# A graph-attention and expert kernel: the scatter products of a chunk are spread 0, 2, 3, 3 over its units, and the last chunk is gathered by pairs of tiles with identity products between them

## The chip, the cores and the metric

The kernel runs on one core of a Trainium2 chip. The metric is device time in microseconds (us) of one execution, as the median of several runs. TensorE (PE in the profile) does the matrix products, with its weight loads shown apart (PEld); VectorE (DVE), ScalarE (ACT) and GpSimd (POOL) do elementwise work; SyncE's queue (SPq) issues nearly all DMAs. All DMAs of the core share 16 DMA engines.

## What is computed

```
x = x + gnn(layernorm(x))                 # x: 32 batches x 256 rows x 256
x = x + ffn(layernorm(x))
gnn: 8-head attention with adjacency mask, output projection, bias
ffn: rows in groups of 16; 64 expert slots (16 experts x 4 sets), 32 wide
  logits = grouped @ controller + tie           # 16 x 64 per group
  perm   = (logits == max over the 16 rows)     # one-hot, per group and slot
  inner  = relu(sum over rows of (grouped @ f1) * perm)
  inter2 = inner @ f2                           # per group and slot: 256 numbers
  result = sum over slots of inter2 * perm      # back to the rows
```

## The kernel before

The first two thirds of the time are the attention, batch by batch. The change touches only the second part, the experts. Its 8192 rows are 64 tiles of 128 rows, in 4 chunks of 16 tiles; a chunk is 4 units of 4 tiles.

**A unit** (`unit`, L714) prepares the experts' input. For one of its four tiles, `select` (L650) multiplies the normalised rows with the one-hot matrix, so that each expert slot gets the row it has chosen; DVE and ACT each copy half of the result out of four PSUM banks (L246, `save_selected`), and the next `select` waits for both copies, since it writes the same banks. In between TensorE does work for later units: `unit_transpose` (L546, two units ahead), `one_hot_transpose` (L566, the next unit) and `logits` (L559, two units ahead). DVE turns the logits into the one-hot matrices (L1067, L1074, L1086).

**The experts** of a chunk (`experts`, L736) are 16 steps of `expand` (L661, with f1) and `contract` (L682, with f2). The result of a step (512 KB) is copied to one of 5 slots of `stage` (DVE L1246, ACT L918) and written to `scratch` in DRAM by `move` (L325), where it lies by group.

**The scatter** brings it back to the rows. The chunk's result is read from `scratch` in another order, by expert slot and for one tile at a time: `gather(c, tile)` (L335, 512 KB per tile, 16 tiles) loads into the same 5 slots. `scatter(c, s)` (L709) multiplies the two tiles 2s and 2s+1 with the transposed one-hot matrices, into the one bank 3, and `finish` (L1204, DVE) adds the result to X, after which `store` (L341) writes it to the output. Eight scatters, s = 0 to 7, serve a chunk. For chunks 0 to 2 they run inside the units of the following chunk; the function `scatters(u)` says which s belong to unit u. Inside a unit the first stands after `select` 0, the second after `select` 2 and, where there is one, the third after `select` 3. DVE has the first `finish` ahead of the copy of `select` 1, the second ahead of the copy of `select` 3, and the third after the one-hot matrices of the unit.

Three waits tie this together. A tile from the sixth on is gathered only when the scatter that read its slot is done: tiles 5 and 6 after scatter 0, 7 and 8 after scatter 1, 9 and 10 after 2, 11 and 12 after 3, 13 and 14 after 4, tile 15 after scatter 5. A scatter after the first waits for the previous `finish`, since both use bank 3. And the one-hot matrices of a unit are written into a region of which the scatter of six units ago must be done. SyncE's queue has, in this order, the chunk's 16 moves, 16 gathers, 8 stores. So every store of a chunk and the first move of the next stand behind gather 15.

**The last chunk** has no following units. Its slots are not reused: `XRlast` holds all 16 tiles, loaded by 4 DMAs of 2 MB (L356), 4 tiles each. `scatter_last(s)` (L695) waits for its DMA where s is even, has four banks in turn, and `finish` and `store` follow.

Of the kernel before, what the change touches and what calls it, by code (L numbers as in the profile page):

```python
# [15 lines left out]
P = 128  # L16
# [7 lines left out]
def gnn_moe_kernel(nc, x, adj, Wq, bq, Wk, bk, Wv, bv, Wo, bo, controller, f1, f2, out):  # L24
# [11 lines left out]
    CT = 16  # L36
    CHUNKS = TILES // CT
    UT = 4
    UNITS = CT // UT
    GPT = P // T  # L40
    CG = CT * GPT
# [26 lines left out]
    with ExitStack() as ctx:  # L68
        def sb(name, shape, dt=F32):
            return ctx.enter_context(nc.sbuf_tensor(name, shape, dt))  # L70

        def sem(name):
            return ctx.enter_context(nc.semaphore(name))
# [7 lines left out]
        ident = sb("ident", [P, P])  # L81
# [66 lines left out]
        XRlast = nc.alloc_sbuf_tensor_at("XRlast", [P, CT, 4, D], F32, offset=floor)  # L148
# [4 lines left out]
        bank = [banks[:, i, :] for i in range(8)]  # L153
# [19 lines left out]
        bo_added = sem("bo_added")  # L173
        bias_ready, bias_done = sem("bias_ready"), sem("bias_done")
        root_done = sem("root_done")
        last_in = [sem(f"last_in{i}") for i in range(4)]
        hT_ready, hT_saved = sem("hT_ready"), sem("hT_saved")
        q_ready, q_saved = sem("q_ready"), sem("q_saved")
        k_ready, k_saved = sem("k_ready"), sem("k_saved")
# [69 lines left out]
        def out_bank(s):  # L249

            return bank[(7, 0, 1, 2)[s % 4]]

        def scatters(u):

            return ((), (0, 1, 2), (3, 4, 5), (6, 7))[u]

        def region(n):

# [2 lines left out]
        def chosen(tile, j):  # L261

            return permT[region(tile // UT)][:, (tile % UT * 4 + j) * 32:(tile % UT * 4 + j) * 32 + 32]
# [10 lines left out]
        def uses_of_slot(s):  # L274

            return (QUADS - s + SLOTS - 1) // SLOTS
# [11 lines left out]
        def _(sp):  # L288
# [62 lines left out]
                move(CHUNKS - 1, q)  # L351
            for i, m in enumerate(moved):
                sp.wait_ge(m, CHUNKS * uses_of_slot(i) * 16)
            for i in range(4):
                rows = slice((CHUNKS - 1) * CG + 4 * GPT * i, (CHUNKS - 1) * CG + 4 * GPT * (i + 1))
                sp.dma_start(XRlast[:, 4 * i:4 * i + 4, :, :].rearrange("p t j d -> p (t j) d"),  # L356
                             scratch[rows, :].rearrange("(c two) (e d) -> (two e) c d", two=2, d=D))\
                    .then_inc(last_in[i], 16)
            for s in range(CT // 2):
# [64 lines left out]
        def _(pe):  # L424
# [260 lines left out]

            def scatter_last(s):

                if s % 2 == 0:
                    pe.wait_ge(last_in[s // 2], 16)
                if s > 3:  # L690
                    pe.wait_ge(fin_done, (CHUNKS - 1) * (CT // 2) + s - 3)
                for tt in range(2):
                    for j in range(4):
                        tile = (CHUNKS - 1) * CT + 2 * s + tt
                        last = nc.tensor.matmul(out_bank(s)[32 * j:32 * j + 32, tt * D:tt * D + D],  # L695
                                                chosen(tile, j), XRlast[:, 2 * s + tt, j, :],
                                                start=True, stop=True)
                last.then_inc(sc_ready, 1)
# [15 lines left out]
            def unit(c, u):  # L714

                n = c * UNITS + u
                ahead = n + AHEAD < CHUNKS * UNITS
                pairs = scatters(u) if c > 0 else ()
                if ahead:
                    unit_transpose(n + AHEAD)  # L720
                select(n, 0)
                if n + 1 < CHUNKS * UNITS:
                    one_hot_transpose(n + 1)
                if pairs:
                    scatter(c - 1, pairs[0])
                select(n, 1)
                if ahead:
                    logits(n + AHEAD)
                select(n, 2)
                if pairs:  # L730
                    scatter(c - 1, pairs[1])
                select(n, 3)
                if len(pairs) > 2:
                    scatter(c - 1, pairs[2])
# [15 lines left out]
                experts(c)  # L750
            for s in range(CT // 2):
                scatter_last(s)


        @block.scalar
# [171 lines left out]
        def _(dve):  # L927
# [279 lines left out]
            def unit(c, u):  # L1207
                n = c * UNITS + u
                ahead = n + AHEAD < CHUNKS * UNITS
                pairs = scatters(u) if c > 0 else ()  # L1210
                save_selected(c, u, 0)
                late_root_steps(c, u, 0)
                if pairs:
                    finish(c - 1, pairs[0])
                save_selected(c, u, 1)
                late_root_steps(c, u, 1)
                if ahead:
                    tied_logits(n + AHEAD)
                save_selected(c, u, 2)
                late_root_steps(c, u, 2)  # L1220
                if pairs:
                    finish(c - 1, pairs[1])
                if ahead:
                    group_maximum()
                save_selected(c, u, 3)
                late_root_steps(c, u, 3)
                if ahead:
                    one_hot(n + AHEAD)
                if len(pairs) > 2:
                    finish(c - 1, pairs[2])  # L1230
# [46 lines left out]
```

## Time and profile before

| | before |
|---|---|
| median of 3 runs | 808.16 us (806.3 to 810.27) |
| the profiled execution | 806.59 us, its span 804.8 us |
| granted TensorE clock, mean | 0.977 |
| PE, DVE, ACT, POOL busy | 90%, 76%, 71%, 16% |
| HBM read, written | 47.78 MB, 41.94 MB |
| first unit's transposes with gathers open to first `expand`: chunks 1, 2, 3 | 591.23 to 627.68, 649.75 to 685.95, 708.01 to 743.63 us |
| gathers of the last chunk issued; last instruction of DVE starts | 770.65; 801.51 us |

The profiled execution took 1.8 us beyond its span, and lies 1.6 us under the median. The span is the time from the first to the last instruction; all times below are counted from its start. "Idle before <-releaser" in brackets says how long the engine stood idle ahead of an instruction and whose end released it. [...]

### The profile page before, as it was taken

Reading aid. Unit: us, or ns where it says so; the run is one execution under the profiler, and the core shown is the slowest. Engines: PE = TensorE matmul, PEld = TensorE weight load, DVE = VectorE, ACT = ScalarE, POOL = GpSimd, SP = SyncE. Lnnn points to the kernel's source line nnn. Section 1 sums busy time; section 2 is a strip of 40 time slices with the busy share of each in tenths; the row PEclk is TensorE's granted clock in tenths of the full one; section 3 lists DMA queues with packets and bytes.
Section 4 is the critical chain, followed back from the end, with each engine's and each line's share of the span. In section 5 each row is a group of like instructions: output and inputs, shape, how many; then the busy total and the mean of one; then the engine's idle time right before and its main releaser. Section 6 shows DMA issues by size and latency. Waiting matters only on the chain.

```text
span 804.8 us, 22451 instructions
## 1 busy us (share of the span) xinstructions
PE 728.1 (90%) x7252; PEld 556.7 (69%) x7252; DVE 612.7 (76%) x2558; ACT 568.3 (71%) x1654; POOL 125.4 (16%) x125
## 2 busy tenths in 40 slices
PE   4789999999999999999999999897888988986925
PEld 3578888888888888888888888765554555553602
DVE  2588998998988989989989989777656656655612
ACT  3499899899999998998998999765553453442500
POOL 1100100000010010001001003436425225200000
PEclk9899999999999999999999999999999999999956
DMA  6476656756765765666567466650589889889889
GB/s 157 105 170 144 160 136 154 172 137 138 171 155 121 170 155 133 161 154 154 139 154 171 112 138 140 151 204 2 211 312 339 329 312 334 338 304 345 345 303 303
DMA packets 102197, 157.60 MB, mean 196 GB/s; under 512 B 12288, under 2 KB 65024, under 8 KB 101888
## 3 DMA queue, kind: packets, MB, share of 16 engines
q1 hardware_dynamic: 99968, 155.56, 67.7%
q10 hardware_dynamic: 2176, 1.31, 0.7%
q8 instruction: 35, 0.57, 0.3%
q14 instruction: 18, 0.15, 0.1%
HBM read 47.78 MB, written 41.94 MB: 111 GB/s over the span
## 4 chain that ended last, share of the span: by engine, by line
PE 71%; DMA 14%; SPq 6%; DVE 5%; issue 2%; ACT 1%; ACTq 0%; DVEq 0%
PE bank L501 13%; PE bank L453 12%; DMA stage<-scratch 7%; PE bank L515 7%; PE bank L488 7%; PE bank L475 6%; PE bank L682 6%; PE bank L538 6%; PE bank L661 5%; SPq L301 4%; DMA XRlast<-scratch 2%; PE bank L446 2%; DMA scratch<-stage 2%; PE bank L650 2%; PE bank L709 2%
## 5 line engine op out<-in xcount | busy, mean ns | idle before, releaser
L826 ACT ACTIVATE Ps<-Ps,nmax 128x256 f32<-128x256 f32 x512 | 255.3, 503 | 23.4 <-DVE nmax L1015 21.7
L1015 DVE CUSTOM_DVE_ANT_0 Ps<-bank,masks 128x256 f32<-128x256 f32 x512 | 199.3, 420 | 27.2 <-issue 25.4
L501 PE MATMUL bank<-ident,Ps 128*128 128x128 f32 x1024 | 145.6, 275 | 2.0 <-DVE PTs L1026 1.5
L501 PEld LDWEIGHTS bank<-ident,Ps 128*128 128x128 f32 x1024 | 115.8, 140 | 20.2 <-issue 12.4
L453 PE MATMUL bank<-hT,WT 128*128 128x256 f32 x512 | 125.2, 389 | 0.8 <-ACT hT L783 0.8
L488 PE MATMUL bank<-stack 128*128 128x256 f32 x512 | 118.0, 332 | 6.2 <-DMA stack<-parts 6.0
L382 POOL TENSOR_TENSOR X<-X,bob 128x512 f32 (+1 forms) x32 | 40.8, 1277 | 431.5 <-ACT hn L791 431.5
L453 PEld LDWEIGHTS bank<-hT,WT 128*128 128x128 f32 x512 | 95.6, 196 | 12.2 <-issue 1.1
L826 ACT ACTIVATION_READ_ACCUMULATOR Ps<-Ps,nmax 128x1 f32 x512 | 98.1, 192 | 0.0
L394 POOL TENSOR_SCALAR h<-X,mv,roots 128x256 f32<-128x256 f32 x64 | 80.1, 1263 | 113.5 <-PE bank L650 85.7
L1026 DVE COPY PTs<-bank 128x512 f32<-128x512 f32 x128 | 87.7, 685 | 4.9 <-PE bank L501 4.8
L488 PEld LDWEIGHTS bank<-stack 128*128 128x128 f32 x512 | 80.5, 191 | 14.1 <-issue 5.0
L246 ACT COPY XS<-bank 128x512 f32<-128x512 f32 x64 | 37.8, 590 | 59.9 <-PE bank L650 59.9
L835 ACT COPY PTs<-bank 128x512 f32<-128x512 f32 x128 | 73.9, 577 | 0.4 <-PE bank L501 0.4
L809 ACT ACTIVATE parts<-bank,few 128x256 fp32r<-128x256 f32 x128 | 53.7, 471 | 26.3 <-PE bank L453 24.3
L515 PE MATMUL bank<-PTs,Vs 128*32 128x256 f32 x1024 | 68.5, 385 | 0.0
L918 ACT COPY stage<-bank 128x512 f32<-128x512 f32 x64 | 37.5, 587 | 42.9 <-PE bank L682 42.9
L1001 DVE SCALAR_TENSOR_TENSOR parts<-bank,few,parts 128x256 fp32r<-128x256 f32 x128 | 58.0, 479 | 8.4 <-ACT parts L809 8.4
L246 DVE COPY XS<-bank 128x512 f32<-128x512 f32 x64 | 44.6, 697 | 26.0 <-PE bank L650 25.9
L475 PE MATMUL bank<-WT,hT 128*128 128x256 f32 x256 | 61.9, 385 | 2.0 <-DVE parts L1001 1.8
L1204 DVE TENSOR_TENSOR X<-X,bank 128x512 f32<-128x512 f32 x32 | 22.0, 688 | 54.7 <-PE bank L695 31.1
L1246 DVE COPY stage<-bank 128x512 f32<-128x512 f32 x64 | 43.9, 691 | 25.1 <-PE bank L682 25.1
(84 smaller groups left out, 1028.8 us busy)
## 6 DMA issues: line engine op xcount, KB each, us to landing
stack<-parts SPq DMA_DIRECT2D x512, 128.0 KB, 2.4
scratch<-stage SPq DMA_DIRECT2D x64, 512.0 KB, 4.0
stage<-scratch SPq DMA_DIRECT2D x48, 512.0 KB, 6.2
X<-in_x SPq DMA_DIRECT2D x32, 256.0 KB, 2.8
out<-X SPq DMA_DIRECT2D x32, 256.0 KB, 4.7
XRlast<-scratch SPq DMA_DIRECT2D x4, 2048.0 KB, 15.9
f1s<-in_L_ffn_f SPq DMA_DIRECT2D x1, 2048.0 KB, 8.0
f2s<-in_L_ffn_f SPq DMA_DIRECT2D x1, 2048.0 KB, 13.9
```

Source lines behind the costliest of these rows:

```text
L246: return copy(XS[:, :, :, first:first + 4].rearrange("p k e (j two) -> p k e j two", two=2), banks[:, 4 + 2 * hf:6 + 2 * hf, 0:2 * P].rear ...
L394: last = nc.gpsimd.tensor_scalar(h2[n % NORMS][:, t, :], xtile(tile), mv2[:, tile, 0:1], roots[:, 1, tile:tile + 1], ALU.subtract, ALU.mult)
L453: last = nc.tensor.matmul(m[:, g * N:g * N + N], WT[:, w, k, g * P:g * P + P], hT[:, k, :], start=(k == 0), stop=(k == KT - 1))
L475: last = nc.tensor.matmul(M[0][:, t * D:t * D + D], hT[:, k, t * P:t * P + P], WT[:, 2, k, :], start=(k == 0), stop=(k == KT - 1))
L488: last = nc.tensor.matmul(s_bank(n)[:, h * N:h * N + N], stack[:, par, j, 0, g * N + t * P:g * N + t * P + P], stack[:, par, j, 1, g * N:g ...
L501: last = nc.tensor.transpose(PTb[h % 2][:, k * N + t * P:k * N + t * P + P], Ps[:, pr % 2, t, h % 2, k * P:k * P + P], ident[:, :])
L515: last = nc.tensor.matmul(Ob[32 * j:32 * j + 32, g * N:g * N + N], Vs[:, par, k, h * DH:h * DH + DH], PTs[:, h, k * N:k * N + N], start=(k ...
L826: last = nc.scalar.activation(Ps[:, pr % 2, t, h, :], Ps[:, pr % 2, t, h, :], ACT.Exp, bias=nmax[:, pr % 2, t, h:h + 1], scale=-1.0, accum ...
L835: nc.scalar.copy(PTs[:, h, :], PTb[h % 2][:, :]).then_inc(pt_act, 1)
L1001: low = nc.vector.scalar_tensor_tensor(parts[:, par, 2 * which + 1, g, :], M[1 - which][:, g * N:g * N + N], (bqs, bks)[which][:, g:g + 1] ...
L1015: last = nc.vector.tensor_tensor_reduce(out=Ps[:, pr % 2, t, h, :], in0=s_bank(n)[:, h * N:h * N + N], in1=masks[:, t, :], scale=1.0, scal ...
L1026: nc.vector.tensor_copy(PTs[:, h, :], PTb[h % 2][:, :]).then_inc(pt_dve, 1)
```

## The change

`scatters(u)` gives units 0 to 3 the scatters (), (0, 1), (2, 3, 4), (5, 6, 7) in place of (), (0, 1, 2), (3, 4, 5), (6, 7). `XRlast` is loaded by 8 DMAs of 1 MB, two tiles each, with a semaphore for each, and `scatter_last(s)` waits for its own. After each of the first seven of these scatters TensorE multiplies the identity matrix with itself 8 times, 128x128 by 128x128, into bank 5, which nothing reads any more.

```diff
-        last_in = [sem(f"last_in{i}") for i in range(4)]
+        last_in = [sem(f"last_in{i}") for i in range(CT // 2)]
...
-            return ((), (0, 1, 2), (3, 4, 5), (6, 7))[u]
+            return ((), (0, 1), (2, 3, 4), (5, 6, 7))[u]
...
-            for i in range(4):
-                rows = slice((CHUNKS - 1) * CG + 4 * GPT * i, (CHUNKS - 1) * CG + 4 * GPT * (i + 1))
-                sp.dma_start(XRlast[:, 4 * i:4 * i + 4, :, :].rearrange("p t j d -> p (t j) d"),
+            for i in range(CT // 2):
+                rows = slice((CHUNKS - 1) * CG + 2 * GPT * i, (CHUNKS - 1) * CG + 2 * GPT * (i + 1))
+                sp.dma_start(XRlast[:, 2 * i:2 * i + 2, :, :].rearrange("p t j d -> p (t j) d"),
...
-                if s % 2 == 0:
-                    pe.wait_ge(last_in[s // 2], 16)
+                pe.wait_ge(last_in[s], 16)
...
                 scatter_last(s)
+                if s + 1 < CT // 2:
+                    for _ in range(8):
+                        nc.tensor.matmul(bank[5][:, 0:P], ident[:, :], ident[:, :], start=True, stop=True)
```

TensorE's order in the last unit of chunk 1 (h is the normalised input, so L546 is `unit_transpose`, L650 a `select`, L566 `one_hot_transpose`, L559 `logits`; L709 on permT is a scatter; L661 is the first `expand`). Before:

```order
L546 MATMUL bank<-ident,h_1_71 128x128 x8
L650 MATMUL bank<-permR,h_3_64 128x128 x8
L566 MATMUL bank<-ident,permT_74 128x128 x4
L709 MATMUL bank<-stage,permT_69 32x256 x8
L650 MATMUL bank<-permR,h_3_64 128x128 x8
L559 MATMUL bank<-h2T,ctl 64x256 x4
L650 MATMUL bank<-permR,h_3_64 128x128 x8
L709 MATMUL bank<-stage,permT_69 32x256 x8
L650 MATMUL bank<-permR,h_3_64 128x128 x8
L661 MATMUL bank<-XS,f1s 32x128 x16
```

The same unit now (the scatter's line is L708):

```order
L546 MATMUL bank<-ident,h_1_71 128x128 x8
L650 MATMUL bank<-permR,h_3_64 128x128 x8
L566 MATMUL bank<-ident,permT_74 128x128 x4
L708 MATMUL bank<-stage,permT_66 32x256 x8
L650 MATMUL bank<-permR,h_3_64 128x128 x8
L559 MATMUL bank<-h2T,ctl 64x256 x4
L650 MATMUL bank<-permR,h_3_64 128x128 x8
L708 MATMUL bank<-stage,permT_69 32x256 x8
L650 MATMUL bank<-permR,h_3_64 128x128 x8
L708 MATMUL bank<-stage,permT_69 32x256 x8
L661 MATMUL bank<-XS,f1s 32x128 x16
```

The last `select` of the chunk was the last thing ahead of the experts; now scatter 7 stands between them, and scatter 5 has come into this unit from the end of the one before. Unit 1 has lost its third scatter to unit 2.

TensorE's order at the end of the program, where the last chunk is scattered, before:

```order
L682 MATMUL bank<-f2s,h2T 128x256 x8
L695 MATMUL bank<-XRlast,permT_67 32x256 x16
L695 MATMUL bank<-XRlast,permT_65 32x256 x16
L695 MATMUL bank<-XRlast,permT_73 32x256 x16
L695 MATMUL bank<-XRlast,permT_74 32x256 x16
```

And now, from the same place (the first three of eight scatters; the last has no identity products behind it):

```order
L682 MATMUL bank<-f2s,h2T 128x256 x8
L694 MATMUL bank<-XRlast,permT_67 32x256 x8
L754 MATMUL bank<-ident 128x128 x8
L694 MATMUL bank<-XRlast,permT_67 32x256 x8
L754 MATMUL bank<-ident 128x128 x8
L694 MATMUL bank<-XRlast,permT_65 32x256 x8
L754 MATMUL bank<-ident 128x128 x8
```

Each pair of scatters that stood together is now two, with 8 identity products behind each.

## Rows read from the trace of the kernel before

**Rows 1.** The page's span in 40 equal slices: busy tenths of TensorE and DMA

```profile
PE   4789999999999999999999999897888988986925
...
DMA  6476656756765765666567466650589889889889
```

**Rows 2.** Chain of waits that ended last, 595 to 805 us: start, us, what

```profile
616.25 5.69 DMA stage<-scratch
...
671.33 4.95 DMA stage<-scratch
677.03 6.50 DMA stage<-scratch
...
778.92 19.02 DMA XRlast<-scratch
```

**Rows 3.** Timeline of TensorE, chunk 1's units 1 to 3: start, us, line

```profile
601.69 0.64 PE L709 MATMUL bank<-stage,permT 128*32 128x256 f32 x8 [0.85 <-DMA stage<-scratch]
...
605.96 0.64 PE L709 MATMUL bank<-stage,permT 128*32 128x256 f32 x8 [0.73 <-DMA stage<-scratch]
...
606.53 0.73 PE L650 MATMUL bank<-permR,h 32*128 32x128 f32 x16
...
609.52 1.09 PE L546 MATMUL bank<-ident,h 128*128 128x128 f32 x8
...
611.20 0.66 PE L566 MATMUL bank<-ident,permT 128*128 128x128 f32 x4
...
615.12 1.07 PE L709 MATMUL bank<-stage,permT 128*32 128x256 f32 x16
...
618.00 0.64 PE L709 MATMUL bank<-stage,permT 128*32 128x256 f32 x8 [0.37 <-DMA stage<-scratch]
...
618.57 1.09 PE L546 MATMUL bank<-ident,h 128*128 128x128 f32 x8
...
627.68 0.54 PE L661 MATMUL bank<-XS,f1s 128*32 128x128 f32 x12 [1.08 <-DVE XS L246]
```

**Rows 4.** Timeline of SyncE's queue: gather 11 (chunk 1's units), gather 15 (chunks 1, 2, 3)

```profile
612.92 0.36 SPq L335 DMA_DIRECT2D stage<-scratch  x1
...
618.70 0.36 SPq L335 DMA_DIRECT2D stage<-scratch  x1
...
677.03 0.36 SPq L335 DMA_DIRECT2D stage<-scratch  x1
...
735.33 0.36 SPq L335 DMA_DIRECT2D stage<-scratch  x1
```

**Rows 5.** Timeline of TensorE: waits for tile 15 (chunk 2), 11 and 13 (chunk 3)

```profile
683.57 0.64 PE L709 MATMUL bank<-stage,permT 128*32 128x256 f32 x8 [0.44 <-DMA stage<-scratch]
...
734.63 0.64 PE L709 MATMUL bank<-stage,permT 128*32 128x256 f32 x8 [0.66 <-DMA stage<-scratch]
...
738.32 0.64 PE L709 MATMUL bank<-stage,permT 128*32 128x256 f32 x8 [1.51 <-DMA stage<-scratch]
```

**Rows 6.** Timeline of the end, 770 to 804.8 us

```profile
778.97 3.64 PE L695 MATMUL bank<-XRlast,permT 128*32 128x256 f32 x32 [13.20 <-DMA XRlast<-scratch]
...
784.99 3.64 PE L695 MATMUL bank<-XRlast,permT 128*32 128x256 f32 x32 [2.38 <-DMA XRlast<-scratch]
...
797.98 3.46 PE L695 MATMUL bank<-XRlast,permT 128*32 128x256 f32 x32 [3.45 <-DMA XRlast<-scratch]
...
801.51 0.69 DVE L1204 TENSOR_TENSOR X<-X,bank 128x512 f32<-128x512 f32 x1 [0.85 <-PE bank L695]
```

**Rows 7.** Stretches of the end: PE, PEld, DVE, ACT, POOL busy; clock, DMA, GB/s

```profile
785.00:788.70 3.70, 3.63 (x32) 1.37 (x32) 0.69 (x2) 0.00 (x0) 0.00 (x0) 0.50 1.10 349
...
790.90:794.30 3.40, 3.31 (x32) 1.38 (x32) 0.69 (x1) 0.00 (x0) 0.00 (x0) 0.50 1.09 348
794.30:797.70 3.40, 0.23 (x4) 0.00 (x0) 0.69 (x1) 0.00 (x0) 0.00 (x0) 1.00 1.09 361
```

**Rows 8.** The page's DMA issues: count, KB each, median us to landing

```profile
scratch<-stage SPq DMA_DIRECT2D x64, 512.0 KB, 4.0
```

## The prediction

> **What bounds the kernel now.** I read the slices first, then the chain of waits, then the timelines of the stretches that the chain names. In the slices TensorE is at nine tenths nearly everywhere; it falls off only in the last quarter, at the three places where a chunk's results are gathered and at the very end, and there the DMA row is mostly at eight or nine [rows 1]. The attention, two thirds of the time, is untouched. The chain says what those places are: gathers of 5 to 6.5 us each, each issued when a scatter ends and landed when another starts, and at the end 19 us of the last big gather [rows 2].
>
> [...] In a **stretch** (from the first transposes of a chunk to its first `expand`; three of them have scatters) TensorE and the gathers take turns: a slot is refilled only after the scatter that read it. [...]
>
> The sum below is made against the profiled execution, 806.59 us (span 804.8). It lies 1.57 us under the median of 808.16; I add that at the end.
>
> **Part 1, the spread of scatters.** No product is added or removed; what moves is scatter 2 (unit 1 to 2) and scatter 5 (unit 2 to 3). Take chunk 1 [rows 3].
>
> - Unit 1 ends without its third scatter. Its last `select` starts at 606.53 and takes 0.73, of which the next instruction overlaps 0.07, so unit 2 begins at 607.2 and not at 609.52. That is 2.3 earlier: 1.0 of products and 1.3 of waits for tiles 4 and 5 and the previous `finish`.
> - Unit 2 keeps three scatters. It took 9.05 (609.52 to 618.57), some 0.6 of it a stop for tile 11 at 618.00. I take off 0.6 and add 0.4, because the first `select` must now wait for the copy of the previous one, on DVE behind a `finish`. That gives 8.9: unit 3 begins at 616.1.
> - Scatter 5 comes after transposes and a `select` (609.52 to 611.20, 1.7) and L566 (0.6), at 618.4. Its second tile is number 11, whose gather waits for scatter 3. Scatter 3, now the second of unit 2, starts 6.0 after the unit's start (615.12 less 609.52, plus the 0.4), at 613.2, and is done 1.1 later. Gather 11 is issued at 614.4 (before: 612.92) and needs 5.1 (before: 618.00) [rows 3, 4], so it lands at 619.5. Scatter 5 is done 0.7 after that, and gather 15 is issued at 620.2, against 618.70 before.
> - From there the order decides. A gather that was waited for needed 4.95 to 6.50 us from its issue; I take 5.8, near the two longer of the three (6.50 from 677.03, which is gather 15 in chunk 2's units, 5.69 and 4.95) [rows 2, 4]. Tile 15 lands at 626.0. Now only the second half of scatter 7 is left, 0.57, and the experts begin at 626.6. Before, the last `select` came after scatter 7, then its copy, which DVE did only after a `finish`, so that `expand`, released by that copy, began at 627.68. **Gain 1.1.**
>
> The same steps in the other two. Chunk 2: gather 15 is issued at 678.5 (before 677.03). Its 6.5 us were queueing, so it lands between 683.6 as before, if the queue ahead of it is as long, and 684.3; at 683.95, `expand` starts at 684.5 against 685.95. Gain 1.45: tile 15 was itself waited for there (683.57), with a `select`, a `finish` and a copy still behind it [rows 4, 5]. Chunk 3 has no transposes in its last two units: tile 11 comes at 735.6 (before 734.63), gather 15 goes out at 736.4 (before 735.33) and lands at 742.2, `expand` starts at 742.8 against 743.63. Gain 0.8 [rows 4, 5]. **Sum 3.4.**
>
> Bounds: with the shortest transit, 4.95, chunks 1 and 3 gain 0.85 more each and chunk 2 0.4: 5.5. With the longest, 6.50, they lose 0.7, 0.7 and 1.0: 1.0 left. Tiles come 1.5 us apart (four in 6.0 at the end [rows 6]), but some pairs are late: tile 1 at 601.69 and tile 3 at 605.96 are 4.3 apart, 1.2 more than two steps [rows 3]. Such a step can now fall on the last pair, with nothing between it and `expand`; in all three it would take 3.6 more: a loss of 2.6. The middle is nearest to the three rows.
>
> What stands behind the later issue costs nothing: in SyncE's queue that is 8 stores and the next chunk's first move, which is not ready before two `expand`s, a `contract` and a copy into the experts. If the stores still filled the queue then, a `stage` copy would wait for its slot; but 16 steps take 22.1 us (627.68 to 649.75 in the table), so five slots leave a move 6.9 us, and it takes 4.0 [rows 8]. DVE's third `finish` of unit 3 (0.69, as in [rows 6]) falls beside the first two expansions. The one-hot matrices of unit u need scatters up to 2u - 1, which are still done by then.
>
> **Part 2, the end.** The bytes of the last gather are the same and its queue is full, so its last landing stays at 797.98. Four more issues on SyncE, 0.36 each as in [rows 4], lie beside a transfer of 27 us. What changes is what follows the landing: two tiles, not four. Four took 3.46 at clock 0.50 [rows 6]; two at the full clock take 1.07, the row of 615.12 [rows 3]. If TensorE is free when they land, and its clock is up, the end comes 2.4 earlier.
>
> Is it free? Pairs land every 3.0 us (six us for four tiles), the first at 776.0 [rows 6]. An identity block is 8 products, that is 16 records of 128 columns. No row shows it; nearest are the transposes, where 8 records take 1.09 and 4 take 0.66, so 0.108 each [rows 3]: 1.7 for sixteen back to back, 1.9 with the change of instruction, which I take, and twice as much if each record had to wait for its own weights. A pair then costs 1.0 + 1.9 = **2.9 at the full clock**, just under the 3.0, and 1.7 + 3.8 = 5.5 at half. So TensorE starts slow, works without a pause, and falls behind until its clock rises. Bursts of 3.6 us (785.0 to 788.7, and one before) with pauses between left the clock at 0.50; after 3.3 us of the third it rose, at 794.3 [rows 7]. I take 5 us, so 781: 0.9 pairs are done by then, 6.1 remain at 2.9, and scatter 7 starts at 798.6, 0.6 late. Gain 1.8. If the clock rises at 779.3 it is 2.4; at 783, 0.8. **1.8.**
>
> [...]
>
> **Sum**: 3.4 + 1.8 = 5.2. 806.59 - 5.2 = 801.4; with the 1.57, **803.0 us**, 0.64% less. About 0.5% (4.0 us) is what a measurement of this kernel can tell from no change.
>
> **Rivals.**
>
> 1. *The wait only moves.* The gathers set the stretches, and scatters done later delay the refills by as much as the order gains; part 1 is nought, part 2 stands: 806.4. For it: the DMA row is at eight to nine, and tiles 11 and 15 are both issued 1.1 to 1.5 later. Against: in chunk 3 the last tile waited for was number 13, with 5.3 us from its landing to `expand` (738.32 to 743.63), more than the two steps to tile 15 [rows 5]. Its near kin, part 1 as said and identity products that eat what the clock gives back, ends at 804.8. Chance of the two together 0.29.
> 2. *The identity products become the bound of the end* (slower). This happens if a pair's cost stays over 3.0 us. At clock 0.50 throughout, seven pairs at 5.5 from 776.0 put scatter 7 at 814.5; it takes 1.8, and the DVE row that stood at 801.51 stands at 816.3, 14.8 later. Less 3.4: **819.6**. For it: two bursts of 3.6 us did not lift the clock [rows 7]. Against: those had pauses (788.7 to 791.0), these have none. Chance 0.06. [...]
> 3. *Each extra transfer of the end pays its own start.* The price here by a row: the shortest gather of 512 KB waited for took 4.95, where tiles follow at 1.5 [rows 2]: 3.45 of start, four times that 13.8, and 803.0 becomes **816.8**. Against: 16 gathers per stretch come at that pace with several on the way. Chance 0.02.
>
> **Numbers.** The forecast has 0.63. Rival 1 with its kin falls within 0.5%; rivals 2 and 3 are slower, with 0.01 for bad landings in all stretches. Likeliest 803.0. The bounds go from a gain of 7.9 (5.5 + 2.4: 800.3) to a loss of 1.8 (2.6 less 0.8: 810.0). I go half a us below the first for the scatter of runs, and leave out rivals 2 and 3 and the top of the bad bounds: 799.8 to 807.4.
>
> **What would show it.** `expand` starting about 35.4, 34.8 and 34.8 us after the chunk's first transposes (before 36.45, 36.20, 35.62), released by TensorE itself, not by a copy; the last wait of each stretch for tile 15. At the end a clock of 0.50 until about 781, then 1.00; identity blocks of 1.9; L694 of 1.07 as the last product; the last landing within 0.5 us of before, counted from the gathers' issue. Wrong would be: a clock that stays at 0.50, blocks over 2 us, a later last landing, or stretches as long as before with the waits on other tiles.

## The result, and the profile after

| | before | with the change |
|---|---|---|
| median | 808.42 us (8 runs, 805.66 to 810.27) | 801.43 us (8 runs, 798.49 to 804.18) |
| ratio, 95% interval | | 0.9914 (0.9889 to 0.9938) |
| the profiled execution, its span | 806.59, 804.8 us | 801.37, 799.5 us |
| chunk 1, first transposes to first `expand` | 36.45 us | 34.33 |
| chunk 2 | 36.20 | 34.44 |
| chunk 3 | 35.62 | 33.46 |
| the end: first gather into `XRlast` issued to end of span | 34.15 | 33.5 |
| mean granted clock | 0.977 | 0.987 |

Faster by 7.0 us; 5.2 were predicted, and 803.0 us. The same kernel run again later (change_again) gave 0.9937 (0.9912 to 0.9963), 801.54 against 806.90 us, so 5.4 us. Both lie in the range given, and the direction is as forecast. How the gain divides is another matter: the stretches gave 6.0 us in this profile where the sum had 3.4, the end 0.65 where it had 1.8. This profile was a favourable one: over the six profiles with the new spread and without filler products the stretches average 34.8 us, over the two with the old spread and full gathers 36.1, so 1.3 each and 3.9 for three. (The spans differ by 5.3 and not by 6.7, since the untouched attention happened to end 1.7 us later in this execution, and what lies between the stretches and the end took 0.3 us less. That is why stretches are compared, not positions.)

TensorE and DVE around the end of chunk 1's stretch, timeline of the changed kernel (start, us, engine, line; in brackets the idle time before and what ended it: TensorE stood idle 0.73 us ahead of 620.95, until a gather landed):

```profile
592.97 1.09 PE L546 MATMUL bank<-ident,h 128*128 128x128 f32 x8
...
608.60 1.09 PE L546 MATMUL bank<-ident,h 128*128 128x128 f32 x8
...
617.31 1.09 PE L546 MATMUL bank<-ident,h 128*128 128x128 f32 x8
...
619.58 0.64 PE L708 MATMUL bank<-stage,permT 128*32 128x256 f32 x8
620.95 0.64 PE L708 MATMUL bank<-stage,permT 128*32 128x256 f32 x8 [0.73 <-DMA stage<-scratch]
...
625.91 0.68 DVE L246 COPY XS<-bank 128x512 f32<-128x512 f32 x1
...
626.84 0.64 PE L708 MATMUL bank<-stage,permT 128*32 128x256 f32 x8 [0.48 <-DMA stage<-scratch]
...
627.30 0.95 PE L661 MATMUL bank<-XS,f1s 128*32 128x128 f32 x28
```

The last copy (625.91, 0.68 us) is over before TensorE starts on tile 15 at 626.84, 0.04 us after its landing, and `expand` follows by 0.46 us with nothing in between; before, it was released by the copy [rows 3]. Chunks 2 and 3 end the same way:

```profile
683.32 0.64 PE L708 MATMUL bank<-stage,permT 128*32 128x256 f32 x8 [0.71 <-DMA stage<-scratch]
...
683.78 1.06 PE L661 MATMUL bank<-XS,f1s 128*32 128x128 f32 x32
...
738.83 0.64 PE L708 MATMUL bank<-stage,permT 128*32 128x256 f32 x8 [0.63 <-DMA stage<-scratch]
...
739.28 1.06 PE L661 MATMUL bank<-XS,f1s 128*32 128x128 f32 x32
```

SyncE's queue in the changed kernel (first issue, time to the last one's end, count):

```profile
597.67 24.33 SPq L335 DMA_DIRECT2D stage<-scratch  x16
...
654.13 23.43 SPq L335 DMA_DIRECT2D stage<-scratch  x16
...
710.84 23.13 SPq L335 DMA_DIRECT2D stage<-scratch  x16
...
766.00 18.90 SPq L356 DMA_DIRECT2D XRlast<-scratch  x8
```

From the first issue to the landing of tile 15 it is 29.17 us (597.67 to 626.84), 29.19 and 27.99. In the kernel before, the same count from the landing records is 29.2, 29.0 and 28.2; for chunk 2 the rows show it, 654.57 to 683.57 [rows 5]:

```profile
654.57 22.82 SPq L335 DMA_DIRECT2D stage<-scratch  x16
```

So tile 15 did not come later although its gather was issued 0.9, 0.6 and 0.4 us later, counted from the first. From its landing to `expand` it was 2.8, 2.4 and 2.4 us before and is 0.5 now in all three: 6.2 us less, where the stretches got 6.0 shorter. Seen from TensorE, the waits for tiles in chunk 1's stretch fell from 3.5 to 2.5 us (waiter, what it waited for, us in total, times, longest; before, then with the change), in chunk 2 from 3.3 to 2.7, in chunk 3 from 5.6 to 3.4:

```profile
PE bank L709 <- DMA stage<-scratch: 3.5, 6, 0.8
```

```profile
PE bank L708 <- DMA stage<-scratch: 2.5, 4, 0.8
```

The chain of waits of the changed kernel has that gather three times, with its transit:

```profile
621.65 5.15 DMA stage<-scratch
...
677.20 6.08 DMA stage<-scratch
...
733.61 5.18 DMA stage<-scratch
```

The end, timeline of the changed kernel:

```profile
771.44 1.93 PE L694 MATMUL bank<-XRlast,permT 128*32 128x256 f32 x16 [9.91 <-DMA XRlast<-scratch]
...
773.30 2.86 PE L754 MATMUL bank<-ident 128*128 128x128 f32 x16
...
776.10 1.07 PE L694 MATMUL bank<-XRlast,permT 128*32 128x256 f32 x16
...
777.10 2.05 PE L754 MATMUL bank<-ident 128*128 128x128 f32 x16
...
793.99 1.07 PE L694 MATMUL bank<-XRlast,permT 128*32 128x256 f32 x16
...
795.13 0.69 DVE L1206 TENSOR_TENSOR X<-X,bank 128x512 f32<-128x512 f32 x1 [2.29 <-PE bank L694]
...
795.85 0.38 SPq L341 DMA_DIRECT2D out<-X  x1
```

And its stretches (PE, PEld, DVE, ACT, POOL busy; clock, DMA share, GB/s):

```profile
771.40:775.00 3.60, 3.56 (x24) 2.28 (x25) 0.69 (x1) 0.00 (x0) 0.00 (x0) 0.50 1.08 352
775.00:779.00 4.00, 4.00 (x42) 3.25 (x41) 0.69 (x1) 0.00 (x0) 0.00 (x0) 1.00 1.09 348
779.00:793.90 14.90, 14.90 (x162) 11.39 (x160) 3.44 (x5) 0.00 (x0) 0.00 (x0) 1.00 1.09 352
```

The identity products did what they were priced at in this profile: after 3.6 us of unbroken work the clock was at 1.00 and stayed until the last product, a scatter with its block comes every 2.98 us, and the last scatter takes 1.07. TensorE never waits for a tile after the first pair: the chain of waits runs through scatters and identity products alone, from 771.44 to the last DVE step at 795.13.

```profile
771.44 1.93 PE bank L694 x16
773.37 2.79 PE bank L754 x16
...
794.06 1.04 PE bank L694 x16
```

But that DVE step, which started 3.29 us before the end of the span in the kernel before [rows 6], now starts 4.37 us before it. A microsecond of the gain was lost behind the last product. The last store takes 3.2 us from its issue to its landing, where it took 2.1 (the DMA view of 795.8 to 799.4 with the change, of 802.2 to 804.7 before):

```profile
out<-X SPq DMA_DIRECT2D x1, 256.0 KB, 3.2
```

```profile
out<-X SPq DMA_DIRECT2D x1, 256.0 KB, 2.1
```

### The profile page after: what moved, and what is told of

Same layout as the page of the kernel before. It is cut to its first block, busy times and chain, and to the rows that moved or that the text cites. A ratio compares the mean times of both kernels' runs of the same rounds, so it can differ in the third digit from the quotient of the medians.

```text
span 799.5 us, 22681 instructions
## 1 busy us (share of the span) xinstructions
PE 738.1 (92%) x7364; PEld 570.4 (71%) x7364; DVE 612.0 (77%) x2558; ACT 568.2 (71%) x1654; POOL 125.2 (16%) x125
## 4 chain that ended last, share of the span: by engine, by line
PE 76%; DMA 11%; SPq 5%; DVE 4%; issue 2%; ACT 1%; ACTq 0%; DVEq 0%
PE bank L501 13%; PE bank L453 13%; PE bank L515 7%; PE bank L488 7%; PE bank L475 6%; PE bank L682 6%; PE bank L538 6%; DMA stage<-scratch 6%; PE bank L661 5%; SPq L301 4%; PE bank L650 2%; PE bank L446 2%; DMA scratch<-stage 2%; PE bank L754 2%; PE bank L708 2%
## 5 line engine op out<-in xcount | busy, mean ns | idle before, releaser
L828 ACT ACTIVATE Ps<-Ps,nmax 128x256 f32<-128x256 f32 x512 | 255.3, 503 | 25.0 <-DVE nmax L1017 23.1
L1248 DVE COPY stage<-bank 128x512 f32<-128x512 f32 x64 | 43.9, 691 | 27.8 <-PE bank L682 27.8
L538 PE MATMUL bank<-WT,OT 128*128 128x256 f32 x256 | 60.6, 379 | 1.4 <-DVE OT L1042 1.4
```

The source lines that it names most:

```text
L538: last = nc.tensor.matmul(M[1][:, t * D:t * D + D], OT[:, g, t * P:t * P + P], WT[:, 3, g, :], start=(g == 0), stop=(g == G - 1))
L828: last = nc.scalar.activation(Ps[:, pr % 2, t, h, :], Ps[:, pr % 2, t, h, :], ACT.Exp, bias=nmax[:, pr % 2, t, h:h + 1], scale=-1.0, accum ...
```

## The experiments

In what follows P is the theory that the gathers of a stretch run at their own pace from the first issue; Q that tile 15 is timed by its own issue and a transit, as the prediction had it; S that the end is bound by the DMA queue, stores included; G that TensorE's waits make the clock fall. Stretches are from one profile each; the end is counted as in the table. The kernels that are not in the table (two_stores, identity16, half_before, half_after) ran once each.

| kernel | stretches, us | end, us | median, us | ratio to before (95%) |
|---|---|---|---|---|
| spread_only | 36.88, 35.16, 35.28 | 34.2 | 805.14 | 0.9956 (0.9932 to 0.9979) |
| end_only | 36.42, 36.47, 35.22 | 33.4 | 807.31 | 0.9993 (0.9976 to 1.0011) |
| no_identity | 33.99, 33.40, 36.26 | 33.4 | 802.38 | 0.9929 (0.9904 to 0.9954) |
| groups_0323 | 33.64, 35.19, 33.24 | 33.7 | 801.04 | 0.9917 (0.9886 to 0.9948) |
| late_two | 37.43, 35.15, 36.84 | 33.5 | 803.97 | 0.9969 (0.9946 to 0.9991) |
| filler | 36.67, 34.78, 36.96 | 33.6 | 802.46 | 0.9936 (0.9912 to 0.9959) |
| filler_both | 34.11, 33.37, 34.81 | 33.5 | 801.18 | 0.9943 (0.9920 to 0.9965) |
| change_again | 34.27, 33.38, 36.64 | 33.4 | 801.54 | 0.9937 (0.9912 to 0.9963) |

### The two parts apart

```diff
-            return ((), (0, 1, 2), (3, 4, 5), (6, 7))[u]
+            return ((), (0, 1), (2, 3, 4), (5, 6, 7))[u]
```

> The kernel before with the scatters 0, 2, 3, 3 alone; the end as before. Theory P (pace): the gathers of a stretch run without a gap at 1.5 us a tile, so tile 15 lands 28 to 29 us after the first gather in any order, and the gain is all that stood behind it: the three stretches are 34.3, 34.4, 33.5 us as with the whole change (before 36.45, 36.20, 35.62), and the time is 6 us under that of before, ratio 0.9925. Theory Q (issue and transit, as predicted): 3.4 us of gain, ratio 0.996, if the profile with the change was a lucky one.

Measured: 0.9956, theory Q's number; theory P's 0.9925 lies outside the interval, and its stretches of 34.3, 34.4 and 33.5 us were missed by 5 us in all. The first was a bad one: tile 1 landed 3.1 us after tile 0, where 1.5 is usual, TensorE waited 2.1 us for it, the clock was at 0.50 from 602.5 to 606.0, and tile 15 landed 31.6 us after the first gather. In chunk 3 the clock fell too, of which more below. The other kernels with the same spread (the change, its repeat, no_identity) put the worth of the spread higher, so 3.5 us (this kernel, by its ratio; its medians differ by 2.4) to 6 (the change's profile) is what can be said. Profiles of single executions differ too much here to settle it closer.

```diff
-            return ((), (0, 1), (2, 3, 4), (5, 6, 7))[u]
+            return ((), (0, 1, 2), (3, 4, 5), (6, 7))[u]
```

> The change without the new spread: pairs of tiles with identity products, scatters 0, 3, 3, 2. As predicted: 1.8 us of gain. Theory S (stores): the last products end 2.2 us sooner, but the stores of the last chunk wait in the DMA queue behind the gathers, and the last store takes 3.2 us from issue to landing, not 2.1, so only 0.7 us of gain, ratio 0.999. The stretches are as before, 36.1 us on average.

Measured: 0.9993, with nought in its interval, and an end of 33.4 against 34.15 us: 0.7 us, as theory S has it. The predicted 0.9978 is still within the interval; the end in the profile speaks against it.

### The change without its identity products

```diff
-                if s + 1 < CT // 2:
-                    for _ in range(8):
-                        nc.tensor.matmul(bank[5][:, 0:P], ident[:, :], ident[:, :], start=True, stop=True)
```

> The change without the identity products: spread and pairs stay. The clock stays at 0.50 over most of the end, so the last scatter takes 1.9 us and not 1.07, but it starts when its tiles land and not 0.25 later: TensorE is done 0.6 us later. If the store backlog (theory S) bounds the end, 0 to 0.5 us of that shows; without backlog all 0.6. Time 0 to 0.6 us over that of the change, ratio 0.992 to the kernel before. If the identity products were worth what the prediction gave them, 1.5 us or more.

The end of its timeline, and the stretch in which it lies:

```profile
797.74 1.94 PE L694 MATMUL bank<-XRlast,permT 128*32 128x256 f32 x16 [1.00 <-DMA XRlast<-scratch]
...
799.74 0.69 DVE L1203 TENSOR_TENSOR X<-X,bank 128x512 f32<-128x512 f32 x1 [2.25 <-PE bank L694]
```

```profile
770.00:800.00 30.00, 15.47 (x128) 4.75 (x128) 5.08 (x8) 0.00 (x0) 0.00 (x0) 0.50 1.03 334
```

The clock stays at 0.50 for all of the end, the last scatter takes 1.94 instead of 1.07, and the end is 33.4 us, no longer than the 33.5 with the products. The DVE step starts 3.7 us before the end of the span (803.4), where with the products it was 4.37: what TensorE saved there the store queue took. Nor does TensorE save it as a rule. Counted from the first gather, the last DVE step starts at 29.1 us in the change's profile, but at 29.7 in its repeat and at 29.4 to 30.4 in the other kernels with 8 products; without them it is 29.8 (here) and 29.9 (filler). In all of these that keep their eight stores the end is 33.4 to 33.7 us. The identity products, though they have the clock at 1.00 from 775.0 us on, are worth nothing that these runs show; what the end gains comes from loading by pairs (34.2 without, in spread_only, 33.4 here).

### Fewer stores, and longer blocks

```diff
-            for s in range(CT // 2):
+            for s in (CT // 2 - 2, CT // 2 - 1):
                 store(CHUNKS - 1, s)
-            sp.wait_ge(out_done, CHUNKS * (CT // 2) * 16)
+            sp.wait_ge(out_done, (CHUNKS * (CT // 2) - CT // 2 + 2) * 16)
```

> The change, with the last chunk's stores 0 to 5 left out (the output lacks 12 of the last chunk's 16 tiles). Theory S: the end, from the issue of the first XRlast gather to the end of the span, is 33.5 us with the change and 34.1 before; without the stores in the queue the last one takes 2.1 us instead of 3.2 and the end is 32.3 us. If TensorE bounds the end, it stays at 33.5.

Measured: last DVE step at 794.68, end of span 798.0, so 3.3 us as in the kernel before, and not 4.37; the last store took 2.2 us: the 1.1 us is the store queue. The end as a whole was 33.0 and not 32.3, since the clock rose 10.1 us after the first gather instead of 9.0, and the products ended 0.6 later:

```profile
794.68 0.69 DVE L1206 TENSOR_TENSOR X<-X,bank 128x512 f32<-128x512 f32 x1 [2.30 <-PE bank L694]
```

```diff
-                    for _ in range(8):
+                    for _ in range(16):
```

> The change with 16 identity products in each of the seven blocks, not 8. A block takes 3.9 us at full clock (2.0 with 8), a pair 4.9, more than the 3.0 between landings: TensorE bounds the end. Seven pairs and the first ones at half clock put scatter 7 some 37 to 39 us after the first gather's issue (27.99 with the change); the end is 43 to 45 us, against 33.5, and the time some 10 us over that of the change. If weight loads or the clock made the blocks free, it would stay at 33.5.

Measured: 815.05 us in one run; the end is 45.3 us.

```profile
799.27 1.07 PE L694 MATMUL bank<-XRlast,permT 128*32 128x256 f32 x16
800.27 3.84 PE L754 MATMUL bank<-ident 128*128 128x128 f32 x32
804.03 1.07 PE L694 MATMUL bank<-XRlast,permT 128*32 128x256 f32 x16
```

Sixteen products cost 3.77 us, a pair 4.76 (799.27 to 804.03), more than the 3.0 between landings. Eight cost 1.98 and a pair 2.98. By these numbers a ninth product, some 0.2 us, would already be too many; the slower rival lay one step away, by the length of a block and not by the clock.

### What the gathers cost: half of each tile

```diff
-                sp.dma_start(XR[:, tile % SLOTS, :, :], by_expert(c, tile)).then_inc(gathered[tile % SLOTS], 16)
+                first = c * CG + GPT * tile
+                half = scratch[first:first + GPT // 2, :].rearrange("(c two) (e d) -> (two e) c d", two=2, d=D)
+                sp.dma_start(XR[:, tile % SLOTS, 0:2, :], half).then_inc(gathered[tile % SLOTS], 16)
```

> The kernel before, but a gather brings only the first half of each tile (256 KB), so that the scatters of chunks 0 to 2 work on old data in the other half. Theory P: without the pace of the gathers the stretches are TensorE's own work, 32.5, 32.5 and 30.1 us (before 36.45, 36.20, 35.62), with no wait for a tile. If the stretches were bound by TensorE and the slots, they stay within 1 us of before.

> The same halving on the kernel with the change (the scatters of chunks 0 to 2 work on old data in half of each tile). Theory P: 31.9, 31.9 and 30.3 us, within 0.7 us of the order before with half gathers: the order of the scatters by itself is worth little, what it saves is work behind the last landing. Theory O (order): the new order is 2 us shorter a stretch here too.

Only the time of these two kernels means anything, since their scatters work on old data in half of each tile. Chunk 1's stretch of the first, then of the second:

```profile
594.00 1.09 PE L548 MATMUL bank<-ident,h 128*128 128x128 f32 x8
...
626.33 1.08 PE L663 MATMUL bank<-XS,f1s 128*32 128x128 f32 x32 [1.08 <-DVE XS L246]
```

```profile
592.25 1.09 PE L548 MATMUL bank<-ident,h 128*128 128x128 f32 x8
...
623.51 1.08 PE L663 MATMUL bank<-XS,f1s 128*32 128x128 f32 x32
```

Measured: 32.33, 32.17 and 29.29 us with the old order, 31.26, 31.07 and 29.37 with the new. In neither does TensorE wait for a tile in the three stretches. With its waits for the copies, its own work is thus 3 to 4 us shorter than the stretches in the new order and 4 to 6 in the old. Without the pace of the gathers the new order saves 1.1, 1.1 and -0.1, some 2.1 in all (theory P had 1.0, theory O 6), and that is the copy that no longer stands ahead of `expand`: the wait of 1.08 in the first row pair is gone in the second. With the pace it saved 6.0 in the change's profile. The larger part of the gain in that profile, some 4 us, is therefore that TensorE's work now lies ahead of the last landing, not behind it.

### Other orders

```diff
-            return ((), (0, 1), (2, 3, 4), (5, 6, 7))[u]
+            return ((), (0, 1, 2), (3, 4), (5, 6, 7))[u]
```

> The change with scatters 0, 3, 2, 3: unit 1 as before, scatter 7 last as in the change. Theory P: tile 15 is still timed by the pace of the gathers, stretches as with the change, 34.1 us on average, time within 1 us of the change. Theory Q: scatter 5 starts some 1.5 us later than with the change, gather 15 is issued at 29.6 us of the stretch, lands 5.2 later, stretches 35.3, time 3.5 us over that of the change.

Measured: tile 15 landed 28.6, 29.8 and 27.7 us after the first gather, stretches of 34.0 on average, the time equal to that of the change. That is P's number; Q's 35.3 and 3.5 us more are excluded. It does not decide between the mechanisms, though, since gather 15 was not issued as late as Q had it: at 28.6, 29.1 and 27.8 us of the stretches, where Q had 29.6 and the change's profile 28.7, 27.9 and 27.8. And in two stretches tile 15 was out of step: it landed 2.4 and 3.5 us after tile 14, where 1.4 is usual. When its gather went out, tiles 13 and 14 were to land within 0.7 and 2.1 us (tile 14 within 3.7 to 5.0 in the kernel before and the change), and then the DMA engines were partly idle (PE, PEld, DVE, ACT, POOL busy; clock, DMA share, GB/s):

```profile
622.10:624.10 2.00, 2.00 (x40) 1.28 (x36) 1.64 (x3) 0.59 (x1) 1.50 (x2) 1.00 0.67 147
678.30:680.80 2.50, 2.50 (x48) 1.58 (x48) 1.95 (x4) 0.88 (x2) 1.52 (x2) 1.00 0.61 148
```

So in these two stretches the pace held only while gathers were outstanding. In chunk 2 gather 15 was issued 24.2 us after the first and tile 15 landed at 29.8, where the change's profile has 23.1 and 29.2: a late issue did make tile 15 late there.

```diff
-            return ((), (0, 1), (2, 3, 4), (5, 6, 7))[u]
+            return ((), (0, 1, 2), (3, 4, 5), (None, 6, 7))[u]
...
-                if pairs:
+                if pairs and pairs[0] is not None:
```

(The last two lines are changed twice, in the unit of TensorE and in that of DVE.)

> The change with units 1 and 2 as before (scatters 0 to 2 and 3 to 5), and in unit 3 scatters 6 and 7 after the third and the fourth select, so that scatter 7 is last as in the change. Theory P: tile 15 lands 28 to 29 us after the first gather again, and the work behind the landing is gone, but units 1 and 2 still wait for early tiles, and unit 3 starts at 27 us of the stretch and has 7.7 us of TensorE's work: 34.7 us on average, 1.4 under before and 0.6 over the change. If only the place of scatter 7 counted, 34.1; if only the relief of unit 1 counted, 36.1 as before.

Measured: 0.9969, that is 2.5 us, 0.7 of it the end, so about 0.6 us a stretch. The profiled execution was the slowest of its twelve (810.44), and in chunks 1 and 3 disturbed, both by the clock (at 0.50 from 607.9 for 3.4 us, from 741.0 for 6.8); chunk 2, undisturbed, has 35.15. The expected 1.4 us a stretch was too much: with 0.7 for the end it gives 0.994, just outside the interval. Tile 15 landed 28.3 us after the first gather in chunk 2, as P has it, but `expand` came 1.9 us after that landing and not 0.5, since TensorE was still busy with unit 3. Scatter 7 last is not enough, TensorE must also have done more by then.

### The clock in chunk 3's stretch

In four of the seven profiles with the change's spread or 0, 3, 2, 3 and no filler the clock fell to 0.50 for 6.8 us in this stretch; so it did in late_two. In the two with the old spread and full gathers it did not, which may be chance. The repeat of the change shows it:

> The change itself, on the chip of the two others. Its time stands at ratio 0.9914 to the kernel before; here between 0.990 and 0.994. In half the profiles the clock falls in chunk 3's stretch.

```profile
731.15 0.64 PE L708 MATMUL bank<-stage,permT 128*32 128x256 f32 x8 [1.99 <-DMA stage<-scratch]
...
734.90 1.94 PE L708 MATMUL bank<-stage,permT 128*32 128x256 f32 x16
```

```profile
728.00:732.00 4.00, 1.86 (x40) 0.78 (x36) 1.27 (x3) 0.59 (x1) 0.00 (x0) 1.00 1.06 348
732.00:735.00 3.00, 2.21 (x36) 1.69 (x36) 1.24 (x2) 0.59 (x1) 0.00 (x0) 0.50 0.97 294
```

TensorE waits 2 us for tile 11, is busy 1.86 of 4 us, and the next scatter takes 1.94 instead of 1.07. The four stretches with a fall average 36.0 us (35.28, 36.26, 35.96, 36.64), the three without 33.6 (33.46, 33.24, 34.08): 2.4 us. Most of it stands behind tile 15: `expand` comes 1.9 to 2.4 us after its landing in the four, 0.5 in the three. Ahead of the falls TensorE had waited 1.1, 1.8, 2.0 and 2.0 us for tile 11, in the three without a fall 1.1, 0.7 and not at all. In chunk 1 the clock fell for 3.4 us in three profiles (spread_only, late_two, filler), each time after a wait of 2.1 to 2.6 us for tile 1; those stretches took 36.9, 37.4 and 36.7 us. In end_only a wait of 2.1 us there brought no fall. Two kernels put products in that gap: filler, which has none at the end, and filler_both, which has those too.

```diff
                 for tt in range(2):
                     tile = 2 * s + tt
+                    if c == CHUNKS - 2 and s > 4 and tt == 1:
+                        for _ in range(3):
+                            nc.tensor.matmul(bank[0][:, 0:P], ident[:, :], ident[:, :], start=True, stop=True)
```

> The change without identity products at the end, but with 3 of them (into bank 0) between the two tiles of scatters 5, 6 and 7 in chunk 3's units. In three of six profiles with the new order the clock fell to 0.50 for 6.8 us in chunk 3's stretch, which was then 35.8 us on average and not 33.6. Theory G (gate): TensorE's wait for tile 11 or 13 brings the fall; with products in the gap the clock stays at 1.00 there and the stretch is 33.6 to 34.0 us. Time as of the change or up to 1.5 us under it, about 800 us. If the falls come from something else, the clock falls again in this profile in one case of two, and the stretch is 35.8.

> The kernel of filler with the 8 identity products at the end as in the change. Theory S: the end is 33.5 us as without them, so the time is that of filler within 0.6 us. Theory G: again no fall in chunk 3's stretch. Otherwise 1.5 us under filler, as the prediction priced the higher clock.

Measured: in neither profile did the clock fall there, which fits theory G, though two without a fall could be chance. But the stretches were 36.96 and 34.81 us, not 33.6 to 34.0, and the times are those of the change. In filler the stretch was long all the same, since its tiles came late (tile 10 was waited for too, and tile 15 landed 30.1 us after the first gather), and each block of three products takes TensorE's time whether there is a gap or not: `expand` came 1.2 us after tile 15 in filler and 1.7 in filler_both, where the change's profile has 0.5. What the filler may save in the clock is not seen in the time. No version here beats the change; groups_0323 equals it.

## Why the prediction was right, and where its terms were off

**The place.** Three stretches and the end bound the kernel, and only they changed. TensorE's work behind the stretch's last landing was the lever, `expand` is now released by TensorE itself right behind scatter 7, and the last wait is for tile 15, all as listed beforehand.

**Part 1, step by step.** In chunk 1 unit 2 began 15.6 us into the stretch (predicted 16.0), unit 3 at 24.3 (24.9), scatter 5 at 26.6 (27.2), its second tile after a wait at 28.0 (28.3), gather 15 was issued at 28.7 (29.0). In chunks 2 and 3 gather 15 was issued at 27.9 and 27.8 (28.8 and 28.4): against the kernel before it was 1.2, 0.6 and 0.5 us later, where 1.5, 1.5 and 1.1 were taken. That delay is the term that was most off. It makes 1.8 of the 2.7 us by which part 1 was too small in this profile. The transit of gather 15 was priced at 5.8 us in chunks 1 and 3 and came to 5.45 in chunk 2; it took 5.15, 5.18 and 6.08, which makes 0.6 more. The last 0.3 is the step from the landing to `expand`, 0.5 and not 0.6.

**Where the sum could have been simpler.** Into the stretch, tile 15 landed at 33.6, 33.8 and 33.2 us before and at 33.8, 33.9 and 33.0 with the change. A landing that stays where it was, with 0.5 us behind it, gives 34.1, 34.3 and 33.7 us for the three stretches, a gain of 6.2 (measured 6.0). The prediction argued so for chunk 2 ("if the queue ahead of it is as long") and then took a later landing. But this is no law of the queue. Over the 36 stretches of the twelve profiles with full gathers, tile 15 landed 27.7 to 31.6 us after the first issue and 4.5 to 6.7 us after its own, and where it was late, its gather was issued late too (26.4 us after the first for the 31.6). These runs do not separate the two ways of counting. In the change's own profile the DMA engines were half idle when gathers 9 and 10 had only just gone out, which they were not in the kernel before (610.65 to 612.15, as long after the first gather; first with the change, then before):

```profile
612.70:614.20 1.50, 1.50 (x26) 0.92 (x24) 1.20 (x3) 0.59 (x1) 1.17 (x1) 1.00 0.53 162
```

```profile
610.65:612.15 1.50, 1.50 (x28) 1.13 (x32) 0.69 (x1) 1.50 (x4) 1.50 (x2) 1.00 1.07 345
```

**What the size hides.** The 3.9 us that the profiles give on average for the three stretches are near the 3.4 of the sum; the run times give 3.5 to 6.3, once 0.7 for the end is taken off. The falls of the clock, 2.4 us each and seen in four of seven profiles, were not named as a risk of part 1. The total of 5.4 to 7.0 us agrees with 5.2 partly by luck: part 1 was too small, part 2 too large.

**Part 2.** In this profile the parts of TensorE came out: 8 identity products stand as 16 records (x16 at 773.30), as taken, blocks of 1.98 (1.9), pairs of 2.98 (2.9), the first pair 4.66 (771.44 to 776.10; 5.5 if the clock had not risen in it), full clock from 775.0, 3.6 us after the first product (5 assumed), scatter 7 at 793.99, 0.25 after its landing (0.6). The wrong step is what follows the landing: "the end comes 2.4 earlier", less 0.6 for the lag, took the way from the last DVE step to the end of the span as unchanged, 3.3 us. The eight stores of 256 KB stand in the same queue behind 8 MB of gathers. While TensorE was late, the queue drained meanwhile; now the last store meets it and takes 1.1 us more. Also the last gather landed 27.74 us after the first issue, not 27.3. So 1.8 became 0.65. Luck was in it too: a pair of 2.98 us can't make up a lag against landings 3.0 us apart. The lag shrank from 1.3 us (scatter 2 at 779.08, its pair landed at 777.75) to 0.3 because one pair, the fifth, came 4.0 us after the one before. In the repeat the clock rose 10.2 us after the first gather and not 9.0, and scatter 7 started 0.95 us after its landing.

**The rivals.** The wait did not only move: TensorE's waits for tiles shrank by 3.7 us in the three stretches of this profile. The identity products are the chain of the end, with a pair of 2.98 of 3.0 us, but did not make it longer than without them; at 16 products the predicted mechanism is there, at 815 us. Nor did each record wait for its own weights, which would have doubled the block: at clock 1.00 the full-height identity records come every 0.12 us (1.98 by 16), with loads of 0.19 each beside them. Four more transfers did not pay a start each: pairs landed 3.0 to 3.3 us apart, all but that fifth one, and the last landed 27.6 to 28.0 us after the first issue in the eleven profiles with eight transfers, 27.3 to 27.4 in the three with four, so 0.1 us for each. The start of 3.45 us with which rival 3 was priced does not show as a cost for each of them. The chances of the prediction, 0.63, 0.29, 0.06, 0.02 and 0.01, add up to 1.01.

## What to carry to other kernels

Look at what stands between the last arrival of a queue of transfers and the work that it holds up, and move it ahead of that arrival. Work out that arrival in two ways, by count and pace from the first issue and by the last issue plus a latency: the first was the better guess in the change's profile, while several gathers were outstanding (tile 15 landed 29.2, 29.2 and 28.0 us after the first issue, before 29.2, 29.0 and 28.2), and it failed where the queue ran nearly empty (tile 15 of groups_0323 came 2.4 and 3.5 us after tile 14, not 1.4). Before you speed up the engine at a kernel's end, look at what is already queued for the step after it: here the last store took 3.2 us and not 2.1. The identity products raised TensorE's clock at the end from 0.50 to 1.00, and gained nothing, since a block takes 1.98 us of TensorE's time and the stores came next (an end of 33.5 us, and 33.4 without them).

## What was not expected of the hardware

**Late steps between tiles.** Tiles land 1.5 us apart, but in every stretch with full gathers one to four of them come 0.4 to 2.0 us late, mostly by about 1 us. Around most such steps the DMA page shows a 16 KB packet on the instruction queue, as here for 600.5 to 602.5 and 619.3 to 622 us of the kernel before, ahead of tiles 2 and 13 (the first of the two):

```profile
q8 instruction: 1, 0.02, 3.6%
```

Of the 16 partial landings of tile 13 the last came about 1 us after the others (fifteen by 620.90, one at 621.93), and so in the last gather of the kernel before (fifteen by 796.93, one at 797.93). With the change such a packet stands at 780.2 us: the pairs that land up to 780.75 are complete within 0.2 us of their fifteenth part, the four after it only 1.0 us after. By their shares the packets ahead of tiles 2 and 13 took 1.15 us (3.6% of 16 engines over 2.0 us) and 1.04 us (2.4% over 2.7). In the twelve profiles with full gathers such a packet had begun within 4 us before the landing in 62 of the 84 steps of over 1.9 us, and in 118 of the 420 of under 1.6. That fits a packet that occupies one of the 16 DMA engines for some 1.1 us, which then stays behind; no run took these packets away, so it is an inference. It does not explain every late step: tile 15 of chunk 1 in groups_0323 came late with no such packet, behind a queue that had run nearly empty.

**The clock fell after partly idle stretches.** In change_again, 1.86 us of work in 4 was followed by 6.8 us at 0.50, and stretches with such a fall were 2.4 us longer than those without. It depends on the execution: the change's own profile was spared. That the wait brings the fall was not isolated: waits of 1.1 to 2.6 us stood ahead of seven of these falls, but only two of 0.74 us ahead of the one in chunk 3 of late_two, and one of 1.1 (the change) and one of 2.1 us (end_only) passed without a fall.
